# Two transformer layers on one core: the first two and the last two steps of the pipeline rearranged

## The reference

```python
# layer 0 (EPS 1e-5)
t1 = layer_norm(x, g1, be1)
x = x + self_attn(t1, mask, Wq, bq, Wk, bk, Wv, bv, Wo, bo)
x = x + (ctx @ Wg.T + bg)
x = x + relu(layer_norm(x, g2, be2) @ W1.T + b1) @ W2.T + b2
# layer 1 (EPS 1e-6)
x = x + mha(layer_norm(x, ln1), same, causal)
y = x + mha(layer_norm(x, ln2), ctx)
out = y + relu(layer_norm(y, ln3) @ w1 + b1) @ w2 + b2
```

## Time and profile before

| | |
|---|---|
| median of 3 runs | 1538.21 us (1537.88 to 1539.03) |
| profiled execution, time | 1535.29 us |
| its span, first to last instruction | 1533.5 us |
| mean granted TensorE clock | 0.985 |
| instructions | 39185 |
| TensorE, VectorE, ScalarE, GpSimd busy | 92%, 76%, 67%, 55% of the span |
| DMA | 187 MB, mean 122 GB/s, all from SP's queue |

### The profile page before, as it was taken

The page is one execution under the profiler, slowest core; times in us unless marked ns, Lnnn a source line. Parts: engine busy times, 40 slices in busy tenths (PEclk is TensorE's granted clock), DMA queues, the critical chain, the costliest instruction groups (busy, mean ns, idle before and its releaser), DMA issues.

```text
span 1533.5 us, 39185 instructions
## 1 busy us (share of the span) xinstructions
PE 1417.8 (92%) x13504; PEld 1169.4 (76%) x13504; DVE 1162.3 (76%) x3862; ACT 1034.0 (67%) x2087; POOL 839.4 (55%) x1144
## 2 busy tenths in 40 slices
PE   3889999999999999998888888889999999999996
PEld 3679989988998988876666666657777777787766
DVE  3888888888888888778778778777777767777642
ACT  4777777777777776566666676676666776666652
POOL 4455555545555565655555455456656566655534
PEclk8999999999999999999999999999999999999998
DMA  5554434334433444544555555453443334443300
GB/s 158 161 143 132 128 113 111 111 111 123 127 112 111 117 117 121 146 121 129 160 156 143 150 145 165 141 164 101 132 123 109 110 105 114 123 131 97 90 15 15
DMA packets 161588, 187.07 MB, mean 122 GB/s; under 512 B 15984, under 2 KB 136176, under 8 KB 161392
## 3 DMA queue, kind: packets, MB, share of 16 engines
q1 hardware_dynamic: 161392, 184.57, 41.8%
HBM read 125.78 MB, written 58.72 MB: 120 GB/s over the span
## 4 chain that ended last, share of the span: by engine, by line
PE 70%; DVE 12%; issue 7%; ACT 6%; POOL 3%; SPq 1%; DMA 1%; DVEq 0%; POOLq 0%; ACTq 0%
PE d_ps L489 28%; PE d_ps L755 10%; PE o_ps L626 9%; PE s_ps L548 7%; PE t_ps L562 7%; PE t_ps L596 4%; DVE prob L961 4%; PE m_ps L496 2%; ACT q_stack L813 2%; DVE o_q L1042 1%; ACT prob_t L805 1%; DVE stats L967 1%; ACT h_f L891 1%; DVE top L946 1%; PE t_ps L600 1%
## 5 line engine op out<-in xcount | busy, mean ns | idle before, releaser
L805 ACT ACTIVATE prob_t<-t_ps 128x384 f32<-128x384 f32 (+1 forms) x512 | 276.4, 547 | 266.6 <-PE t_ps L596 157.2
L548 PE MATMUL s_ps<-k_stack,q_stack 96*128 96x256 bf16 (+1 forms) x1536 | 285.2, 267 | 38.6 <-DVE top L961 23.4
L796 ACT ACTIVATE prob<-prob,neg_max 128x256 f32<-128x256 f32 x512 | 231.0, 506 | 66.6 <-DVE neg_max L961 64.8
L1189 POOL TENSOR_TENSOR h_lo<-h_f,h_hi 128x512 fp32r<-128x512 f32 x128 | 164.4, 1285 | 123.4 <-DVE h_hi L1082 123.4
L961 DVE CUSTOM_DVE_ANT_0 prob<-s_ps,bias_sb 128x256 f32<-128x256 f32 x512 | 194.4, 416 | 30.7 <-PE s_ps L548 27.6
L548 PEld LDWEIGHTS s_ps<-k_stack,q_stack 96*128 96x128 bf16 x1536 | 116.0, 98 | 131.2 <-issue 46.4
L946 DVE TENSOR_REDUCE top<-s_ps 128x2 f32<-128x512 f32 x256 | 170.3, 681 | 51.3 <-PE s_ps L548 49.7
L596 PE MATMUL t_ps<-q_stack,k_stack 108*128 108x256 bf16 (+1 forms) x1024 | 201.6, 263 | 4.1 <-ACT q_stack L813 4.1
L961 DVE CUSTOM_DVE_ANT_0 prob<-s_ps,causal 128x128 f32<-128x128 f32 (+1 forms) x512 | 156.9, 351 | 48.5 <-PE s_ps L548 47.7
L626 PE MATMUL o_ps<-prob_t,v_sb 128*17 128x256 f32 (+1 forms) x3072 | 192.0, 368 | 0.0
L489 PE MATMUL d_ps<-x2t_hi,w_hi 128*128 128x256 f32 x512 | 155.8, 304 | 5.4 <-POOL x2t_lo L1189 3.4
(11 more groups left out here) (126 smaller groups left out, 3923.8 us busy)
## 6 DMA issues: line engine op xcount, KB each, us to landing
parts<-q_part SPq DMA_DIRECT2D x96, 192.0 KB, 2.3
parts<-k_part SPq DMA_DIRECT2D x96, 192.0 KB, 2.3
q_stack<-parts SPq DMA_DIRECT2D x96, 192.0 KB, 3.2
k_stack<-parts SPq DMA_DIRECT2D x96, 192.0 KB, 3.3
q_stack<-parts SPq DMA_DIRECT2D x96, 128.0 KB, 3.1
k_stack<-parts SPq DMA_DIRECT2D x96, 128.0 KB, 3.1
ct_kept<-ct_hl SPq DMA_DIRECT2D x16, 512.0 KB, 3.6
x_in<-x_mid SPq DMA_DIRECT2D x32, 256.0 KB, 3.3
```

The source lines that it names most:

```text
L548: last = mm(s_ps[:, h % 2, q * S:q * S + n], q_stack[0:ROWS, t.par, head_of(t, h), q * P:(q + 1) * P], k_stack[0:ROWS, t.par, head_of(t, h ...
L796: last = nc.scalar.activation(prob[:, h % 4, q, :], prob[:, h % 4, q, :], ACT.Exp, bias=neg_max[:, h % 4, q:q + 1], scale=-1.0)
L805: nc.scalar.activation(prob_t[:, h % 8, 0:n], t_ps[:, h % 2, 0:n], ACT.Exp, scale=-1.0)\
L1189: g.tensor_tensor(dst, a, b, ALU.subtract).then_inc(done, 1)
```

## The change

Beginning:
- ScalarE runs one Exp on the tile that GpSimd sets first, ahead of its wait for the constants.
- `keep_busy(n)`: n matmuls of 128x128 bf16 into `s_ps`, whose result nobody reads: 28 ahead of the flip of step -2, 48 behind it, 40 behind the flip of step -1.
- `split_at` of step -1 is (4, 6): q's last parts come ahead of k's first, and SP writes q's parts one slot earlier.
- The six `k_stack` DMAs of step -1 go to ScalarE's queue (slot 7).
- `choose_rows` is called for buffer 0 in slot 2 and for buffer 1 in slot 5.

End, step 48: W1 in slots 7 to 10, its groups 2 and 3 into `s_ps`, waiting no more for the relu two groups before; O in slot 12, W2 in slots 12 to 15. ScalarE writes `h_hi` itself (a second relu), VectorE's cast goes; `ot_lo` is VectorE's (`minus`).
Step 49: W1 of all groups in slot 5, into `s_ps` and `t_ps`, by `first_product`: the matmuls with `x2t_hi` of groups 0 and 1 go first, on the new semaphore `end_hi`, which comes after the first half of the affine; then those with `x2t_lo`. `x2t_lo` and `h_lo` are VectorE's, `h_hi` ScalarE's. W2 goes by pairs of f (both token halves of a pair before the next), each part waiting for its own h_lo.

```diff
+FILL_SPLIT_AT = (4, 6)
...
+TAIL_AT = 0, (7, 8, 9, 10), 12, (12, 13, 14, 15)
...
+        self.o_at = O_AT[self.prev.p] if self.prev else None
+        self.tail, self.end = s == NTASK, s == NTASK + 1
+        if self.tail:
+            self.flip_at, self.w1_at, self.o_at, self.w2_at = TAIL_AT
+        if self.end:
+            self.w2_at = (9, 10, 11, 12)
+        if s == -1:
+            self.split_at = FILL_SPLIT_AT
...
+        def mlp_bank(st, n):
+            if st.end:
+                return (s_ps if n < 2 else t_ps)[:, n % 2]
+            return (d_ps if n < 2 or not st.tail else s_ps)[:, n % 2]
...
+                        if st.s == -1:
+                            continue
...
+            def keep_busy(n):
+
+                for _ in range(n):
+                    mm(s_ps[:, 0, 0:P], ident_bf[:, :], ident_bf[:, :], start=True, stop=True)
...
+            def first_product(st, n, phase):
+
+                bank = mlp_bank(st, n)
+                for f in range(2):
+                    c = slice((2 * n + f) * P, (2 * n + f + 1) * P)
+                    for k in range(KC):
+                        pairs = (((w1_hi, x2t_hi), (w1_lo, x2t_hi)), ((w1_hi, x2t_lo),))[phase]
+                        for i, (w, x) in enumerate(pairs):
+                            last = mm(bank[:, f * S:(f + 1) * S], w[:, k, c], x[:, k, :],
+                                      start=phase == 0 and f == 0 and k == 0 and i == 0,
+                                      stop=phase == 1 and f == 1 and k == KC - 1)
+                return last
...
-                if h in st.w1_at and has(st.old, MLP):
+                if h == st.w1_at[0] and st.end:
+                    pe.wait_ge(end_hi, 1)
+                    pe.wait_ge(u_done.sem, u_done.after(st.old))
+                    pe.wait_ge(e_done.sem, e_done.after(st.old))
+                    first_product(st, 0, 0)
+                    first_product(st, 1, 0)
+                    pe.wait_ge(x2t_l.sem, x2t_l.after(st.old))
+                    for n in range(4):
+                        if n >= 2:
+                            first_product(st, n, 0)
+                        first_product(st, n, 1).then_inc(w1_mm.sem, 1)
+                elif h in st.w1_at and has(st.old, MLP) and not st.end:
...
-                    else:
+                    elif not st.tail:
                         pe.wait_ge(h_done.sem, h_done.after(st.old, n - 1))
+                    elif n == 2:
+                        pe.wait_ge(u_done.sem, u_done.after(st.prev))
...
+                        if not st.end:
+                            pe.wait_ge(h_done.sem, h_done.after(st.old, 1 if st.tail else 3))
+                        elif st.older:
+                            pe.wait_ge(y_done.sem, y_done.after(st.older))
+                    if st.end:
+                        pe.wait_ge(h_l.sem, h_l.after(st.old, part + 1))
+                    else:
+                        pe.wait_ge(h_l.sem, h_l.after(st.old, 2 if st.tail and part == 0 else min(part + 3, 4)))
...
+                    if st.end:
+                        terms = [(t, 2 * m + f, n) for m in range(FT // 2) for t in range(TT) for f in range(2)
+                                 for n in range(3)]
...
+                        opens = f == 0 and n == 0 and (t == 0 or not st.end)
+                        closes = f == FT - 1 and n == 2 and (t == TT - 1 or not st.end)
+                        last = mm(d_ps[:, 0, t * D:(t + 1) * D], lhs, rhs, start=opens, stop=closes)
...
+                if h == st.xf_at and st.s == -2:
+                    keep_busy(28)
...
+                    if st.s < 0:
+                        keep_busy((48, 40)[st.s + 2])
...
+            act.wait_ge(causal_made, 1)
+            nc.scalar.activation(table_row[:, :], minus_half[:, :], ACT.Exp).then_inc(table_in, 1)
...
-            def choose_rows():
-                for par in range(2):
...
+            def choose_rows(par):
...
+            def affine(outs, col_g, col_b, done, first=None):
 
                 for out_t in outs:
+                    if first and out_t is not outs[0]:
+                        last.then_inc(first, 1)
...
+                    affine((tf_b,) if st.old.p == 0 else (x2t_hi, tf_b), c, c + 2, x2t_f, end_hi if st.end else None)
...
+                if h == 2 and st.s == -1:
+                    choose_rows(0)
                 if h == 5 and st.s == -1:
-                    choose_rows()
+                    choose_rows(1)
+                if h == 7 and st.s == -1:
+                    t = st.nxt
+                    for m in range(KC):
+                        act.wait_ge(k_written[m].of(t), k_written[m].after(t))
+                        act.sem_inc(passed, 1)
+                        row = 0
+                        for _, n in RUNS:
+                            act.dma_start(k_stack[row:row + n * HD, t.par, 8 * m:8 * m + 8].rearrange("r h s -> r (h s)"),
+                                          parts[t.par, 1, m, 0:n].rearrange("j d h s -> d j (h s)"))\
+                                .then_inc(stacked[m].of(t), 16)
+                            row += n * HD
...
-                        act.wait_ge(h_h.sem, h_h.after(st.old, n - 1))
+                        if not (st.tail or st.end):
+                            act.wait_ge(h_h.sem, h_h.after(st.old, n - 1))
                         act.wait_ge(h_l.sem, h_l.after(st.old, n - 1))
+                    for f in range(2 if st.tail or st.end else 0):
+                        c = C_B1 + FT * MLP.index(st.old.p) + 2 * n + f
+                        last = nc.scalar.activation(h_hi[:, 2 * n + f, :], mlp_bank(st, n)[:, f * S:(f + 1) * S],
+                                                    ACT.Relu, bias=cols_sb[:, c:c + 1])
+                    if st.tail or st.end:
+                        last.then_inc(h_h.sem, 1)
...
+            def minus(dst, a, b, done):
+
+                v.tensor_tensor(dst, a, b.bitcast(F32), ALU.subtract).then_inc(done, 1)
...
+                if h == st.flip_at + 2 and st.end:
+                    dve.wait_ge(x2t_f.sem, x2t_f.after(st.old))
+                    minus(x2t_lo[:, :, :], tf_b[:, :, :], x2t_hi[:, :, :], x2t_l.sem)
...
-                if h - 2 in st.w1_at and has(st.old, MLP):
+                if h - 2 in st.w1_at and st.end:
+                    n = st.w1_at.index(h - 2)
+                    dve.wait_ge(h_done.sem, h_done.after(st.old, n + 1))
+                    minus(h_lo[:, 2 * n:2 * n + 2, :], h_f[:, n % 2], h_hi[:, 2 * n:2 * n + 2, :], h_l.sem)
+                if h - 2 in st.w1_at and has(st.old, MLP) and not (st.tail or st.end):
...
+                    if st.tail:
+                        dve.wait_ge(ot_h.sem, ot_h.after(st.prev))
+                        minus(ot_lo[:, :, :], o_f[:, :, :], ot_hi[:, :, :], ot_l.sem)
...
-                if h == st.flip_at + 2 and has(st.old, MLP):
+                if h == st.flip_at + 2 and has(st.old, MLP) and not st.end:
...
+                if h - 2 in st.w1_at and has(st.old, MLP) and not st.end:
                     n = st.w1_at.index(h - 2)
-                    pool.wait_ge(h_h.sem, h_h.after(st.old, n + 1))
+                    if st.tail:
+                        pool.wait_ge(h_done.sem, h_done.after(st.old, n + 1))
+                    else:
+                        pool.wait_ge(h_h.sem, h_h.after(st.old, n + 1))
...
-                if has(st.prev) and h == (12 if st.prev.p == 0 else st.norm_at + 1):
+                if has(st.prev) and h == (12 if st.prev.p == 0 else st.norm_at + 1) and not st.tail:
```

More of the change, by code:

```diff
@@ L207, in two_layers @@
         later = sb("later", [P, P], BF16)
+        table_row = sb("table_row", [P, TT])
         one_hot = sb("one_hot", [P, CH])
@@ L513, in bank_1_free @@
                 if has(st.old, MLP) and not has(st.nxt, KEYED):
-                    pe.wait_ge(h_done.sem, h_done.after(st.old))
+                    pe.wait_ge(h_done.sem, h_done.after(st.old, 2 if st.tail else 4))
                 elif not st.nxt:
                     pe.wait_ge(x2_done.sem, x2_done.after(st.old))
+            def first_product(st, n, phase):
[9 more added lines that the diff above has]
+                return last
             def by_token(bank, sources, opens=True, closes=True):
@@ L709, in slot @@
                             pe.wait_ge(x2_done.sem, x2_done.after(st.old))
-                    else:
+                    elif not st.tail:
                         pe.wait_ge(h_done.sem, h_done.after(st.old, n - 1))
+                    elif n == 2:
+                        pe.wait_ge(u_done.sem, u_done.after(st.prev))
                     for f in range(2):
                         c = slice((2 * n + f) * P, (2 * n + f + 1) * P)
-                        last = product(d_ps[:, n % 2, f * S:(f + 1) * S],
+                        last = product(mlp_bank(st, n)[:, f * S:(f + 1) * S],
                                        [(w1_hi[:, k, c], w1_lo[:, k, c], x2t_hi[:, k, :], x2t_lo[:, k, :])
@@ L734, in slot @@
```

(32 more changed lines are left out.)

6 lines of the change are left out of this document (3 added, 3 removed).

## The result

| kernel | median us | range | profiled execution | its span |
|---|---|---|---|---|
| before | 1538.28 | 1537.88 to 1539.03 | 1535.3 | 1533.5 |
| after | 1517.63 | 1516.72 to 1519.06 | 1518.18 | 1516.4 |

The ratio is 0.9875, with a 95% interval from 0.9858 to 0.9891: faster by 1.3%. The forecast was 1527.0 with a range from 1521.5 to 1533.2. So the question of this case is where some 9 us come from that no step of the sum had.

A forecast was written before the change was run, and what follows sets the result against it. TensorE, busy 92% of the span, was taken as the bound, with serial chains at both ends. Gains of 5.2, 0.4 and 5.6 us sum to 11.2; from the median 1538.2 that gave 1527.0 us, range 1521.5 to 1533.2.

The forecast's parts named there:

- The middle: Everything between steps -1 and 48: left out of the forecast as untouched, so no term in the sum.
- Beginning, 5.2 us forecast: Steps -2 and -1: gain of 5.2 us, ends 2.5 and 6.2, mostly the smaller of the mask's and k's matmuls' gains.
- the table load: Beginning, ScalarE: an early Exp puts the 1.28 us load into idle time, so q's matmuls can start at 13.5 us.
- the small matmuls' price: Beginning, TensorE: 0.11 us each at half clock and 0.06 at full; 28 take 3.1 us and end before the flip.
- the pace of full clock at q: Beginning, TensorE: full clock in q's first matmul at 13.5 us; q and k take 3.1 us for 5.5.
- ScalarE's price of a DMA: Beginning, k stack: each of ScalarE's six DMA issues costs SP's 0.63 us, with ends 0 and 3.3.
- the mask: Beginning, SP: goes out at 28.8 us for 34.98, lands at 34.1 for 40.28, 6.2 us earlier.
- the DMA engines are the bound: Rival, stack of the beginning: full DMA engines make the mask later by 1.3 us; beginning 3.7, total 1528.5; chance 0.17.
- the second rival: The clock doesn't follow: falls again before step 0, half clock in the tail; beginning 2.0, end 3.0, 1533.2; chance 0.12.
- Step 48, 0.4 forecast: End: value products end near 1495.5 us, mostly lost again on VectorE and GpSimd; 0.4 us gain, ends -1.1 and 2.1.
- my bound of -1.1: Step 48: the low end of its gain, in us, for a second stretch at half clock.
- Step 49, 5.6 forecast: End: last product 13.6 us after the flip for 19.3, ScalarE pacing; 5.6 us gain, ends 4.1 and 6.0.

The follow-up runs named there:

- p32: The kernel before with one unused tile of 32 bytes per partition ahead of one_hot, no instruction changed: 1527.42 us, ratio 0.9936.
- after_far: The changed kernel with table_row allocated behind causal, as the last tile, so that no other tile moves: 1527.12 us, ratio 0.9932.
- start_far: The kernel before with only the beginning of the change, table_row behind causal, steps 48 and 49 as before: 1533.8 us, ratio 0.9974.
- after_ksp: The changed kernel with all twelve stack DMAs of step -1 on SP again: 1516.63 us, ratio 0.986.
- nofill: The changed kernel without the 116 small matmuls: 1518.06 us, ratio 0.9874.
- after_xo: The changed kernel with 64 unused bytes ahead of tf_a and 64 ahead of q_f, moving tf, xt, c_in and ct: 1514.29 us, ratio 0.9856.
- after_xt: The changed kernel with 64 unused bytes ahead of tf_a and 64 ahead of table_row, moving xt, ct, stacks, v_sb and prob: 1513.59 us, ratio 0.9855.
- xt_notail: after_xt with step 48 in its old order: 1516.13 us, ratio 0.9853.
- notail: The changed kernel with step 48 in its old order, step 49 changed: 1518.4 us, ratio 0.9868.

## Why the prediction was wrong

**The middle is what failed.** The step reads: the change touches steps -2, -1, 48 and 49 alone, so I leave the middle. Its instructions are the same, but its tiles are not where they were. The diff shows it in one line, `table_row = sb(...)`, inserted ahead of `one_hot`; I costed the tile's Exp and not its place. p32 puts the place alone at 0.9936, after_far the instructions alone at 1527.1 us, where I had 1527.0 for them. That agreement is luck in part. Of after_far's 11.2 us between the profiled executions the beginning brings 3.7 for 5.2, step 48 -0.4 for 0.4, step 49 6.1 for 5.6, the steps between 0.2, and 1.5 are the half-clock stretch between tasks 45 and 46, which no term had.

**Beginning, 5.2 us forecast; 2.3 in after, 3.7 in after_far, 3.0 in start_far.** Right were the table load (-1.28: the affine starts at 10.13, 0.12 us behind the flip's end). The activation of `table_row` starts at 2.02, 0.01 us behind the load, as before the change (11.74, behind a load that ends at 11.73). The Trainium skill (ScalarE: Activation LUTs, "What ACT_TABLE_LOAD costs") adds a drain of some 1.38 us to each load; the trace doesn't agree, here as little as before. Right too were the small matmuls' price (28 in 3.15 us for 3.1), the pace of full clock at q (13.21 for 13.5) and ScalarE's price of a DMA (0.65 for 0.63).

Two steps failed, and each alone would have kept the beginning under 5.2. One is the mask: issued at 28.02 for 28.8, it was used at 36.64 for 34.1. I gave it the 5.28 us that it took behind a queue that issued one DMA every 0.63 us; in the kernels where two queues issue it takes 8.5 to 9.1 us. That is the rival "the DMA engines are the bound", at about twice its price. The Trainium skill (DMA: Bandwidth & Descriptors, "Issuing engines are not separate DMA queues") says that DMAs of different issuing engines run on the same 16 DMA engines, and that a second issuer saves only sequencer time; the trace agrees (DMA share 0.96 to 1.12 in the rows above, and after_ksp loses nothing). In after_far, start_far, nofill and after_ksp the chain goes through the mask.

The other is the clock, the second rival, which gave the beginning 2.0. In after it fell again at 31 us, ahead of step 0, and k's matmuls end at 38.78, where I had 36.2 at full clock and 38.4 at half: here the chain goes through them and not through the mask. Over the nine profiled kernels with this beginning or a variant of it (nofill, after_ksp), the time at half clock ahead of the first `x` goes with where that lies: 11.6 to 14.4 us and 85.8 to 86.1 (after_xo, after_far, after_xt), 14.7 to 15.3 and 86.7 to 87.0 (after_ksp, start_far), 17.9 to 18.5 and 87.1 to 87.5 (xt_notail, nofill, after, notail). The kernels with the old beginning don't order that way, and their first `x` lies anywhere from 88.5 to 90.7 us, so one trace of each side tells little about a term of 2 or 3 us; what moves it there is open. nofill shows as much: its mask is used 2.2 us later than after's and its first `x` comes 0.1 us earlier. One reading of the earlier trace rows was of the pace and not of the granted clock: 2.4 GHz "near 20.2" is where the matmuls go from 5 to 7 in a microsecond to 10, while the clock row of before stands at 1.00 from 0 to 23 us.

**Step 48, 0.4 forecast, -1.28 in the trace.** The last value products end 1.9 us earlier against `x2t_hi`, not 3.3: after has a half-clock stretch of 6.8 us at 1475.2, before one of 3.4 at 1487.9. From there to O it takes 6.6 us for 6.0: `ot_hi` takes 1.37 for 0.99 and `ot_lo` 1.69, both beside a subtraction of GpSimd (1.26); for `ot_lo` I took 0.69, the price without a neighbour. In the timeline of after:

```profile
1488.01 1.37 DVE L1187 CAST ot_hi<-o_f 128x512 fp32r<-128x512 f32 x1
1489.41 1.69 DVE L1075 TENSOR_TENSOR ot_lo<-o_f,ot_hi 128x512 fp32r<-128x512 f32 x1
...
1502.43 0.69 DVE L1075 TENSOR_TENSOR x2t_lo<-tf_b,x2t_hi 128x512 fp32r<-128x512 f32 x1 [1.71 <-ACT tf_b L888]
```

The value fell just outside the ends I gave (-1.1 to 2.1). The other traces say that the order itself is worth little either way: this stretch takes 26.6 to 27.1 us in the five kernels in which it was read with the old order (before, p32, start_far, notail, xt_notail), and 26.4 to 27.0 in four with the new (after_xt, nofill, after_xo, after_far). The two others with the new order, after and after_ksp, take 27.93 and 28.00, and they alone of the eleven are at half clock for 10.2 us of it and not for 6.8 (mean granted clock 0.82, where after_xt and after_far have 0.87). So the missing 1.3 us are most likely one half-clock stretch more, which is what my bound of -1.1 stood for; why it came in these two isn't shown.

**Step 49, 5.6 forecast, 6.15 measured.** From the flip: `x2t_hi` 1.5 for 1.7, W1 ends 7.5 for 7.5, ScalarE's four groups 5.94 us for 6.72, `y_sb` 13.15 for 13.6. Right in mechanism and size: the granted clock of after stays at 1.00 from there to the last product, as I had thought likely, where before is at half clock from 1515.2 to 1518.6. My own terms from F + 11.1 on (0.7 and 1.5) add up to F + 13.3, nearer than the 13.6 that I wrote.

**The range** ended at 1521.5 because every bound in it came from the two ends, and the one thing it left out had the size of all of them. They don't reach 1521.5 either: 1538.2 less 6.2, 2.1 and 6.0 is 1523.9, and the other 2.4 us were my "a little".

## What to carry to other kernels

Ahead of a prediction, list what the change allocates and which tiles it moves: an unused tile of 32 bytes moved this kernel's time by 0.6%, as much as all edited instructions. When a change brings more or less than its instructions explain and the difference grows evenly over untouched steps, compare the pace of the same matmuls, and run the kernel before with a pad of the same size. With two pads a kernel whose bound is TensorE can be tried for a better distance between its operands for some unused bytes; here that brought perhaps 3 to 4 us more. And where one trace of each side is compared, count the half-clock stretches in it first: one of them, in or out, is 1.5 us here and belongs to no edit.

## What the runs showed of the hardware

- The pace of this kernel's 4-byte matmuls of 256 columns depends on the distance, within a partition, between the tile of the activations (`h`, `x2t`, `ot`, `xt`, `ct`) and that of the weights. Busy time by count for W2: 0.1352 us before, 0.1306 with 32 bytes more, 0.1325 with 64 (171.50 us, 1294 matmuls), 0.1350 with 96 (171.66, 1272), 0.1335 with 128, 0.1320 with 160, 0.1353 with 256. Moving both tiles together by 32 bytes changes nothing (0.1353). With 32 bytes more by moving the weights by 96 and `h` by 128 it is 0.1324, so the distance isn't all.
- A DMA on ScalarE's queue costs ScalarE 0.65 us; with ScalarE and SP issuing together, a mask load took 8.5 to 9.1 us to use, alone behind SP's 5.3 to 5.4.
- 28 matmuls of 128x128 in bf16 take 3.15 us, 0.11 each, in the kernel's first dense work, though the granted clock already stands at 1.00 there, so the clock row alone doesn't tell the pace. From 11 us on it is 21 and 22 of them in a microsecond, under 0.05 each:

```profile
6.00:7.00 1.00, 1.00 (x12) 1.00 (x10) 0.85 (x4) 0.00 (x0) 0.00 (x0) 1.00 1.08 436
...
12.00:13.00 1.00, 1.00 (x22) 1.00 (x18) 1.00 (x1) 1.00 (x2) 1.00 (x1) 1.00 0.00 0
```

- VectorE's subtraction of 128x512 takes 0.69 us alone (step 49) and took 1.69 the one time that it ran beside GpSimd (step 48).
